# A megakernel's attention heads: high half of the weights split on ScalarE, query rows duplicated by DMA

## The reference

```python
x = x + xattn(layernorm(x), ctx)           # cross-attention over 4096 rows of context
x = x + attn(layernorm(x), ...)            # 128 heads, the part that is changed
x = x + ffn8bit(layernorm(x), ...)         # 1024 -> 4096 -> 1024, weights quantized per row

# attn: b=1, s=256, 128 heads of 8 content dims and 64 rope dims
c_q, c_kv = x @ Wq_down, x @ Wkv_down                      # 256 x 128
q_c = (c_q @ Wq_up).reshape(b, s, 128, 8)
q_r = (x @ Wq_rope).reshape(b, s, 128, 64)                 # 1024 x 8192 weights
k_c, v_c = (c_kv @ Wk_up), (c_kv @ Wv_up)                  # as q_c
k_r = x @ Wk_rope                                          # 256 x 64, shared by the heads
scores = (q_c . k_c + q_r . k_r) / sqrt(72)
out = softmax(scores) . v_c;  return out.reshape(b, s, 1024) @ Wo
```

## Time and profile before

| | before |
|---|---|
| median of 3 runs | 990.26 us |
| profiled execution, its own time | 988.92 us |
| its span in the trace | 986.9 us |
| TensorE matmul busy | 905.3 us (92%) |
| VectorE busy | 735.0 us (74%) |
| ScalarE busy | 606.8 us (61%) |
| GpSimd busy | 474.8 us (48%) |
| granted TensorE clock, mean | 0.966 of full speed |

### The profile page before, as it was taken

The page is one execution under the profiler, slowest core; times in us unless marked ns, Lnnn a source line. Parts: engine busy times, 40 slices in busy tenths (PEclk is TensorE's granted clock), DMA queues, the critical chain, the costliest instruction groups (busy, mean ns, idle before and its releaser), DMA issues.

```text
span 986.9 us, 18928 instructions
## 1 busy us (share of the span) xinstructions
PE 905.3 (92%) x6783; PEld 826.4 (84%) x6783; DVE 735.0 (74%) x1150; ACT 606.8 (61%) x1046; POOL 474.8 (48%) x312
## 2 busy tenths in 40 slices
PE   5999999899997999999999999986489999799997
PEld 5997888778886789999999998965389999698996
DVE  6456667654437568889999998876888889888954
ACT  3414443455525478888888887873467787466652
POOL 0220000234426697767676766741176676266573
PEclk9999999989998999999999999998599999799998
DMA  6566676576662778665655555435042442224211
GB/s 263 224 219 242 246 277 234 213 299 255 256 192 81 212 236 265 193 186 165 192 179 168 183 178 189 161 131 203 0 170 100 158 170 86 85 87 172 93 77 44
DMA packets 80006, 174.79 MB, mean 177 GB/s; under 512 B 7584, under 2 KB 57536, under 8 KB 77376
## 3 DMA queue, kind: packets, MB, share of 16 engines
q1 hardware_dynamic: 78928, 171.72, 50.6%
q10 hardware_dynamic: 1008, 2.13, 0.6%
HBM read 161.51 MB, written 11.53 MB: 175 GB/s over the span
## 4 chain that ended last, share of the span: by engine, by line
PE 43%; DVE 11%; ACT 4%; issue 4%; POOL 3%; DMA 2%; DVEq 0%; SPq 0%; ACTq 0%; POOLq 0%
PE bank L51 10%; PE bank L53 9%; PE bank L52 9%; PE bank L1178 3%; PE bank L1207 3%; PE bank L1208 2%; PE bank L1774 2%; PE bank L1575 2%; PE bank L1223 1%; POOL W_all L1921 1%; DVE sx L1036 1%; ACT bank L1337 1%; DVE hT L1687 1%; ACT ring L1622 1%; DVE am L1402 1%
## 5 line engine op out<-in xcount | busy, mean ns | idle before, releaser
L51 PE MATMUL bank<-act_all,W_all 128*128 128x256 f32 (+1 forms) x512 | 157.1, 307 | 7.6 <-DVE act_all L2050 4.6
L849 POOL TENSOR_TENSOR wl<-ring,wh 128x1024 fp32r<-128x1024 f32 x68 | 161.5, 2395 | 0.0
L51 PE MATMUL bank<-act_all,wh 128*128 128x256 f32 x512 | 144.8, 283 | 4.3 <-POOL wl L849 2.1
L53 PE MATMUL bank<-act_all,W_all 128*128 128x256 f32 (+1 forms) x512 | 146.4, 286 | 0.0
L52 PE MATMUL bank<-act_all,wh 128*128 128x256 f32 x512 | 144.6, 283 | 0.0
L53 PE MATMUL bank<-act_all,wl 128*128 128x256 f32 x512 | 144.0, 281 | 0.0
L458 POOL TENSOR_TENSOR xa_WT_l<-ring,xa_WT_h 128x1024 fp32r<-128x1024 f32 x16 | 41.3, 2606 | 187.9 <-ACT xa_WT_h L453 187.9
L1921 POOL TENSOR_TENSOR W_all<-rnd,W_all 128x512 fp32r<-128x512 f32 x72 | 93.2, 1306 | 60.0 <-ACT W_all L1849 59.9
L846 POOL CAST wh<-ring 128x1024 fp32r<-128x1024 f32 x68 | 68.8, 1041 | 98.9 <-PE bank L53 87.9
L1397 DVE TENSOR_TENSOR pl<-bank,ph 128x512 f16<-128x512 f32 x128 | 88.0, 688 | 34.3 <-ACT ph L1347 31.5
L51 PEld LDWEIGHTS bank<-act_all,W_all 128*128 128x128 f32 x512 | 99.0, 193 | 9.7 <-issue 6.3
(11 more groups left out here) (239 smaller groups left out, 2586.7 us busy)
## 6 DMA issues: line engine op xcount, KB each, us to landing
ring<-in_ctx_dram SPq DMA_DIRECT2D x16, 2048.0 KB, 7.9
ring<-in_L_attn_Wq_rope_dram SPq DMA_DIRECT2D x32, 1024.0 KB, 6.6
ring<-in_L_ffn_W_dram SPq DMA_DIRECT2D x15, 2048.0 KB, 7.7
panel<-in_L_ffn_W_dram SPq DMA_DIRECT2D x48, 512.0 KB, 4.2
w1p<-in_L_ffn_W_dram SPq DMA_DIRECT2D x16, 512.0 KB, 3.8
ring<-in_L_xattn_Wq_dram SPq DMA_DIRECT2D x2, 2048.0 KB, 11.6
ring<-in_L_xattn_Wk_dram SPq DMA_DIRECT2D x2, 2048.0 KB, 7.8
opv<-stage SPq DMA_DIRECT2D x32, 128.0 KB, 1.7
```

What stands on the lines that cost most here:

```text
L51: pe.matmul(out, lh, rh, start=start, stop=False, skip_group_check=True)
L53: return pe.matmul(out, ll, rh, start=False, stop=stop, skip_group_check=True)
L849: pool.tensor_tensor(half_of(l, i), half_of(r, i), f32(half_of(h, i)), ALU.subtract).then_inc(w_lo, 1)
```

## The change

Three things are done to the heads stage.

1. The high half of the first half of each group's weights is made on ScalarE (`high_w`), at the start of ScalarE's iteration; GpSimd copies the second half only, and does both subtractions, the first of which now waits for ScalarE. The same for group 0 in the block ahead.
2. `high_q` writes only `qrope`, with two copies per pair. Rows 0 to 63 of `qmix` are filled from `qrope` by four DMAs per group on SP's queue (`duplicate`), the first pair's after the reload of outputs, the second pair's after `store_content` and ahead of the loads of W1 rows and weights. `scores_q` waits for them.
3. The shift in the exponent moves out of `max_rows` and into the exponential's bias, a column of constants (`exp_shift`) that GpSimd fills once.

```diff
-            qq = [sb(ml, f"qq{i}", [P, 2, GROUP, T], F32R) for i in range(QBUF)]
-            qrope, qmix = ([q[:, i, :, :] for q in qq] for i in range(2))
+            qmix = [sb(ml, f"qmix{i}", [P, GROUP, T], F32R) for i in range(QBUF)]
...
+            def high_w(act, g):
+
+                landed(act, g % 2, USE_ROPE + g // 2)
+                act.activation(half_of(wh[g % 2], 0), half_of(rope_raw(g % 2), 0), ACT.Copy).then_inc(w_hi, 1)
+
             def split_w(pool, g):
 
                 landed(pool, g % 2, USE_ROPE + g // 2)
                 h, l, r = wh[g % 2], wl[g % 2], rope_raw(g % 2)
-                for i in range(2):
-                    pool.tensor_copy(half_of(h, i), half_of(r, i)).then_inc(w_hi, 1)
-                for i in range(2):
-                    pool.wait_ge(w_hi, g * 2 + i + 1)
-                    pool.tensor_tensor(half_of(l, i), half_of(r, i), f32(half_of(h, i)), ALU.subtract).then_inc(w_lo, 1)
+                pool.tensor_copy(half_of(h, 1), half_of(r, 1)).then_inc(w_hi2, 1)
+                pool.wait_ge(w_hi, g + 1)
+                pool.tensor_tensor(half_of(l, 0), half_of(r, 0), f32(half_of(h, 0)), ALU.subtract).then_inc(w_lo, 1)
+                pool.wait_ge(w_hi2, g + 1)
+                pool.tensor_tensor(half_of(l, 1), half_of(r, 1), f32(half_of(h, 1)), ALU.subtract).then_inc(w_lo, 1)
...
+                    pool.memset(exp_shift[:, :], SHIFT).then_inc(filled, 1)
...
+                    high_w(act, 0)
                     for n in range(KT):
...
+                qrope = [sb(hd, f"qrope{i}", [P, GROUP, T], F32R) for i in range(QBUF)]
...
+                    def duplicate(g, pair):
+
+                        b = g % QBUF
+                        sp.wait_ge(q_hi, g * GROUP + 2 * pair + 2)
+                        for s in range(2):
+                            h = 2 * pair + s
+                            sp.dma_start(f32(qmix[b][0:ROPE, h, :]),
+                                         f32(qrope[b][s * ROPE:(s + 1) * ROPE, h, :])).then_inc(dup_ready[b][pair], 16)
+
...
+                        if valid(g + 2):
+                            duplicate(g + 2, 0)
                         if 0 <= g + 2 < 6:
                             store_content(sp, 1 + (g + 2) // 2, (g + 2) % 2)
+                        if valid(g + 2):
+                            duplicate(g + 2, 1)
...
                         if k0 == 0 and g:
-                            pe.wait_ge(q_cp, (g - 1) * 2 + pair + 1)
                             pe.wait_ge(q_lo, (g - 1) * GROUP + 2 * (pair + 1))
...
                         if h % 2 == 0:
-                            pe.wait_ge(q_hi, n + 1)
-                        else:
-                            pe.wait_ge(q_cp, n // 2 + 1)
+                            pe.wait_ge(dup_ready[b][h // 2], (g // QBUF + 1) * 2 * 16)
...
                 def heads_scalar(act):
+                    def next_w(g):
+
+                        if weights(g):
+                            if g >= 2:
+                                act.wait_ge(q_ready, (g - 1) * 2)
+                            high_w(act, g)
+
...
-                        b, h = g % QBUF, 2 * pair
-                        act.activation(qq[b][0:ROPE, :, h, :], bank[pair][0:ROPE, 0:T].unsqueeze(1).to_broadcast([ROPE, 2, T]),
-                                       ACT.Copy).then_inc(q_hi, 1)
-                        act.activation(qmix[b][0:ROPE, h + 1, :], bank[pair][ROPE:P, 0:T], ACT.Copy).then_inc(q_cp, 1)
-                        act.activation(qrope[b][ROPE:P, h + 1, :], bank[pair][ROPE:P, 0:T], ACT.Copy).then_inc(q_hi, 1)
+                        for s in range(2):
+                            r = slice(s * ROPE, (s + 1) * ROPE)
+                            act.activation(qrope[g % QBUF][r, 2 * pair + s, :], bank[pair][r, 0:T], ACT.Copy).then_inc(q_hi, 1)
...
-                                       bank[2][0:GROUP, 0:T].unsqueeze(1).to_broadcast([GROUP, GROUP, T]), ACT.Copy,
-                                       bias=SHIFT / RSQRT).then_inc(m_row, 1)
+                                       bank[2][0:GROUP, 0:T].unsqueeze(1).to_broadcast([GROUP, GROUP, T]), ACT.Copy).then_inc(m_row, 1)
...
-                        act.activation(bank[5 + h % 2][:, :], bank[5 + h % 2][:, :], ACT.Exp, scale=RSQRT).then_inc(ex_ready, 1)
+                        act.activation(bank[5 + h % 2][:, :], bank[5 + h % 2][:, :], ACT.Exp, scale=RSQRT,
+                                       bias=exp_shift[:, 0:1]).then_inc(ex_ready, 1)
...
                     for g in range(FIRST, NG):
+                        next_w(g + 3)
                         exps(g, 0)
                         high_p(g, 0)
```

More of the change, by code:

```diff
@@ L795, in build @@
             vrest = onat
+            exp_shift = sb(ml, "exp_shift", [P, 1])
             krope = sb(ml, "krope", [P, 2, T], F32R)
             kmix = sb(ml, "kmix", [P, QBUF * GROUP, T], F32R)
-            qq = [sb(ml, f"qq{i}", [P, 2, GROUP, T], F32R) for i in range(QBUF)]
-            qrope, qmix = ([q[:, i, :, :] for q in qq] for i in range(2))
+            qmix = [sb(ml, f"qmix{i}", [P, GROUP, T], F32R) for i in range(QBUF)]
             nmax = [sb(ml, f"nmax{i}", [P, QT, GROUP]) for i in range(2)]
@@ L831, in store_content @@
                                  f32(part[i][:, tiles, :])).then_inc(stored[u], 16)
-            w_hi, w_lo = sem("w_hi"), sem("w_lo")
+            w_hi, w_hi2, w_lo = sem("w_hi"), sem("w_hi2"), sem("w_lo")
             wo_up, wo_hi, wo_pool, wo_dve = [sem("wo_up0"), sem("wo_up1")], sem("wo_hi"), sem("wo_pool"), sem("wo_dve")
@@ L885, in _ @@
                         pool.memset(V16[:, kt, :, 3 * HEAD:VW], 1.0).then_inc(filled, 1)
-                    pool.wait_ge(filled, 2)
+                    pool.memset(exp_shift[:, :], SHIFT).then_inc(filled, 1)
+                    pool.wait_ge(filled, 3)
                     split_w(pool, 0)
@@ L988, in build @@
             rsum = sx2
-            q_ready, q_hi, q_cp, q_lo = sem("q_ready"), sem("q_hi"), sem("q_cp"), sem("q_lo")
+            q_ready, q_hi, q_lo = sem("q_ready"), sem("q_hi"), sem("q_lo")
             mix_ready = [sem(f"mix_ready{b}") for b in range(QBUF)]
+            dup_ready = [[sem(f"dup_ready{b}_{p}") for p in range(2)] for b in range(QBUF)]
             mx_ready, nm_ready, nt_ready, m_row = sem("mx_ready"), sem("nm_ready"), sem("nt_ready"), sem("m_row")
```

## The result

The changed kernel takes 998.01 us (median of twelve runs, 993.44 to 1006.99) against 989.80 us for the kernel before (median of twelve, 987.58 to 992.56): a ratio of 1.0101, 95% interval 1.0078 to 1.0125. The forecast of 992.3 was 5.7 us too low; the time lies inside the range, in its slower part. The profiled execution of the changed kernel took 1001.59 us, span 999.6, so it is one of its longer ones, 12.7 us over the profiled one of before. Its runs also spread over 13.5 us, those of before over 5. Seventeen more executions of the changed kernel, the profiled one among them, have a median of 1000.74 (993.36 to 1004.84), so the price may be nearer 11 us than 8.

What follows compares the result with a forecast made beforehand. TensorE was taken to set the pace, VectorE close behind. Profiled 988.9 + 2.9 (middle) - 0.5 (start) - 0.3 (tail) = 991.0; 1.34 more for the median gave 992.3 us, own range 989 to 995, 8-in-10 range 982 to 1000.

Steps and rivals of the forecast that it cites:

- What the moved copy does to VectorE: Heads stage: GpSimd's subtractions wait for ScalarE's copy; op 0 groups +5.8, ops 1 and 3 -1.35, op 2 -2.25, ot_low +0.7.
- Head copies on ScalarE: Heads stage, per pair: one copy of 0.59 and two of 0.38 become two of 0.38.
- the lead: Heads stage: second pair's exponential starts 0.6 us earlier on ScalarE, VectorE's last low_p of the group 0.45 earlier.
- Query rows by DMA: Heads stage, SP's queue: four new 64 KB copies per group, 3.9 us allowed for landing; cost 0, moved loads too.
- next first pair: Row copies issued at 521.2, just behind the weight load: landing at some 524 against a need of 526.
- the row copies come late: Rival, heads stage: first pair lands over 3.9 us behind issue, TensorE waits in every group; 38 us, 1030; chance 0.1.
- the forecast's +2.9 for the middle: Middle of the heads stage: -1.35 + 5.8 - 2.25 + 0.7 = +2.9 us.
- Start: Before and at the start of the heads stage: GpSimd's chain shorter, -2.1 at best, +4 at worst; -0.5 taken.
- the start is bound by DMA: Rival, start of the heads stage: new copies stand behind content stores, +4 instead of -0.5, 996.8; chance 0.15.
- The sum: Whole kernel: 988.9 + 2.9 - 0.5 - 0.3 = 991.0 us profiled, 992.3 for the median.
- behind it: Tail behind the middle of the stage, the op 2 of group 30: -0.3 us.
- if scores_q waits for DMA in the middle: Sign against the forecast: in the trace after, TensorE waits for a DMA at scores_q in the stage's middle.

Runs made afterwards that it cites:

- Weights alone: Only the high half of the weights moved to ScalarE, against the kernel before; 997.44 us, ratio 1.0092.
- bias-only kernel: Only the exponent's shift made a column operand of the exponential, against the kernel before; 989.05 us, ratio 1.0003.
- Rows only: Only the query rows copied by DMA, weights on GpSimd and shift in max_rows, against the kernel before; 996.78 us, ratio 1.0094.
- the changed kernel with the combine later: Changed kernel with the combine operation put behind the second maximum instead of ahead of it; 993.74 us, ratio 1.0049 to the kernel before.

## Why the prediction was right and wrong

*What the moved copy does to VectorE: right.* Op 0 was forecast at 2.37 and takes 2.50 to 2.53 in five groups, 1.79 in the sixth, which a late transfer had pushed back. Ops 1 and 3 at 0.41 take 0.41 to 0.42, but for the two behind an ot_low; op 2's groups were forecast at 10.1, and the two that show it clean take 9.94 and 9.95. The price per op 0 group, 1.12, stands open in the changed kernel: in the late group of 645.00, without a transfer to wait for, it is 10.78 - 9.52 = 1.26, and four others with waits for transfers of 0.44 to 0.84 take 10.77 or 10.78 as well. The two groups behind an ot_low take 11.29 instead of 10.97, +0.6 together for a forecast of +0.7. Op 0 ends with GpSimd's first subtraction, not with its second, as assumed. The Trainium skill (SBUF — State Buffer, "Who interferes with whom") states it as a rule: a VectorE instruction with two SBUF inputs contends with a GpSimd instruction that reads SBUF. The 2.50 and the 0.41 above agree, and so does the reciprocal with its one input, which takes 1.74 in every group under a subtraction of GpSimd's.

*Head copies on ScalarE, and the lead: right in direction.* Weights alone has no lead, and an op 0 group there is 11.31 - 9.60 = 1.71 over its floor; with the lead it is the 1.26 above. That the exponential with a bias column takes 0.66 instead of 0.59, 0.27 per group of four, I had left out; the bias-only kernel shows that this costs nothing.

*Query rows by DMA: the step that failed.* It said "Cost 0" of the row copies, and "Cost 0" of the loads that now stand behind duplicate(1). For the loads I asked when ScalarE wants them, and that was right: in the middle ScalarE never waited for W, and GpSimd did (13.7 us in 12 waits) only ahead of a subtraction that waits for ScalarE anyway. For the copies I allowed 3.9 us and took the quiet landing, and a quiet landing is indeed 1.9 to 2.0. What I left out was the third party: the content of the next group, issued right behind the moved loads. Before, it had 7 us of distance from them; now it has 2, and takes 8.8 us to land where TensorE wants it after some 7.3 (440.18 to 449.89 - 2.39). My sentence on the next first pair (issued "just behind this load instead of into an empty queue", landing 2 us early) counted the W load as landed in 6.6. But the moment at which it's issued in even groups is also that of W1 and the store, and it took 10.5. So the pair was issued with the load in flight, and took 3.2 to 6.3. I had written the worst landing of 6.5 into the rival "the row copies come late" at a chance of 0.1 and in all 29 groups. It is partly true: content and copies are late in the even groups alone. I had also priced a wait at its length, and three of them cost 1.8 us more each by the clock. Rows only measures the step: +7.5 us for a forecast of about nothing.

*Why both together cost no more than one.* The +7.5 and the +8.2 fall largely in the same even groups, where TensorE's waits for the transfer and for the maxima behind op 0 don't add: a wait of 0.44 to 0.84 for the transfer shortens the later one for the maxima, and the group takes 10.78 either way. It is the transfers that op 0 hides, in four of its six groups, and in the sixth (g = 20, 13.19) it is the other way round. They show in groups without op 0: 10.33 to 10.76 long for g = 2, 4 and 6, 13.67 and 13.33 for g = 10 and 18. Against the forecast's +2.9 for the middle, the op 0 groups without g = 20, the adds, the other op 2 groups and the ot_low groups come out about as said, 1.0 us below it in all; the six groups named here stand 12.3 us over it, the clock's 5.3 among them. Part of the rest is the start.

*Start: direction right, size off.* The first attend comes 2.6 us earlier instead of 0.5, a little past the bound of -2.1 that I gave from GpSimd's chain. Weights only has 1.5 of it. The rival "the start is bound by DMA" was wrong, although transfers do come late in these groups: one wait of 1.64 for the content at 348.17.

*The sum.* For the profiled execution: start -2.6 for -0.5, middle +14.2 for +2.9, behind it +1.1 for -0.3; +12.7 for +2.1. The medians differ by 8.2. That the median lies in the outer range is in good part luck: it is outside the 989 to 995 of the forecast proper, and a larger miss was averted by the start, and by the overlap of the two prices, neither of which I had reckoned with. What I said would prove it wrong, "if scores_q waits for DMA in the middle", is what happened.

*What stays open.* Odd groups run at 9.52 where the kernel before, and weights only, have 9.60, and rows only 9.57 to 9.70; which of the removed waits of TensorE gives these 0.08 isn't settled. Nor is how the DMA engines share their time between a load and a copy, or why the runs of the changed kernel spread so; that a different number of waits is followed by the lower clock in each would fit, but no trace of the other executions shows it. Nor is it settled which waits bring the clock down: one of 3.22 us in the changed kernel with the combine later (449.46) didn't. An order in which loads, content and copies all keep clear of one another wasn't found; with W1 and W apart in time, in different groups, wasn't tried.

## What to carry to other kernels

When an edit moves a large load past small transfers, list every transfer issued while it's in flight, not only those of the edit, and give each the loaded landing time; another issuing queue didn't shield it here. Price a wait of TensorE at more than its length where the clock may fall behind it. Where two small losses fall in the same groups, measure each part alone: their prices don't add, and undoing one shows less than its own price (4.3 us with both parts in, 11.1 with the weights part alone). A VectorE operation with both inputs in SBUF that shares its time with GpSimd belongs behind the instruction that the critical engine waits for: moving the combine by a line made the kernel before 0.45% faster, more than half of it through the reciprocal, which has one input and was merely in the way.

## What the hardware showed that I had not expected

- A copy of 64 KB within SBUF lands in 1.9 to 2.0 us alone and in 3.2 to 6.3 with 1.5 MB of loads issued 5.7 us ahead of it; with the loads on the other queue, 5.2 to 5.6 ahead, in 4.0 to 6.7. With 128 KB instead of 1024 KB of W it is back at 2.0. A 1024 KB load takes 6.6 at the median of before, and 7.7 to 10.5 with 512 KB issued just ahead of it and stores and content just behind.
- SP's time for an issue goes with what it issued just before: a row copy takes 0.46 us when SP comes from a wait and 0.60 behind another copy, and a load right behind one takes 0.59 where it took 0.36 to 0.40 before. Now and then an issue takes far longer, up to 1.83 here (406.03) and up to 1.86 in the kernel before (418.76), so this isn't the new traffic. Two of the three worst groups have such an issue of the W load just ahead of their content (1.36 at 437.27, 1.53 at 520.54).
- Behind waits of 1.9 to 2.4 us TensorE's granted clock fell from 1.00 to 0.50 in three groups, and each time the group's matmuls took 1.8 us longer.
- Moving both loads to a queue of their own cost 26 us more (1024.00 for 998.01) at the same size. Some 9 us of that stand at the stage's start, where the loads went out later; in the middle the moment was nearly the same.
